# Last stream of an eight-phase kernel: more chunks of the down product split, weights turned earlier, one wait added on GpSimd

## The reference

```python
# phase 6: 16 heads of 8; half of the heads see every second row and are upsampled
x = x + jnp.tanh(g_xattn[3]) * _L3_xattn_ref(_layernorm(x), ctx_1024, ctx_1024, ...)
# phase 7: 32 experts of width 64, the best 8 (in the best 4 of 8 groups), and a shared expert of width 128
logits = h @ gate_w.T ; scores = sigmoid(logits) ; combine = 2.5 * normalised top 8
g = silu(einsum('th,eih->tei', h, w_gate)) ; u = einsum('th,eih->tei', h, w_up)
routed = einsum('tei,ehi->th', g * u * combine[:, :, None], w_down)
shared = (silu(h @ sh_gate.T) * (h @ sh_up.T)) @ sh_down.T
x = x + jnp.tanh(g_ffn[3]) * (routed + shared)
```

## Time and profile before

| | |
|---|---|
| three runs, median (lowest to highest) | 833.05 us (830.68 to 836.3) |
| the profiled execution | 832.02 us, of which the span is 830.0 us |
| PE, DVE, POOL, ACT busy | 802.3, 499.0, 450.2, 439.2 us (97, 60, 54, 53% of the span) |
| mean granted PE clock | 0.994 of full speed |
| phase 7 on PE | from 668.40 us to the end |

### The profile page before, as it was taken

The page is one execution under the profiler, slowest core; times in us unless marked ns, Lnnn a source line. Parts: engine busy times, 40 slices in busy tenths (PEclk is TensorE's granted clock), DMA queues, the critical chain, the costliest instruction groups (busy, mean ns, idle before and its releaser), DMA issues.

```text
span 830.0 us, 13575 instructions
## 1 busy us (share of the span) xinstructions
PE 802.3 (97%) x4407; PEld 557.1 (67%) x4407; DVE 499.0 (60%) x1419; ACT 439.2 (53%) x801; POOL 450.2 (54%) x432
## 2 busy tenths in 40 slices
PE   4999999999999999999999999999998999999998
PEld 4876667677767666665666666656564576677776
DVE  6865535393845545335555858676756647486744
ACT  2443555656546343324667676756654654546543
POOL 5375655466654536375546444354554357575463
PEclk9999999999999999999999999999998999999999
DMA  8303030315423242442234141312213042515161
GB/s 317 111 27 103 6 97 1 109 58 161 140 66 101 53 136 67 137 122 49 71 97 106 51 108 40 100 48 58 60 43 95 10 143 65 152 54 167 54 183 60
DMA packets 44871, 75.29 MB, mean 91 GB/s; under 512 B 8993, under 2 KB 9633, under 8 KB 44673
## 3 DMA queue, kind: packets, MB, share of 16 engines
q1 hardware_dynamic: 44656, 74.42, 30.5%
q10 hardware_dynamic: 144, 0.01, 0.0%
HBM read 56.11 MB, written 1.51 MB: 69 GB/s over the span
## 4 chain that ended last, share of the span: by engine, by line
PE 86%; DVE 8%; ACT 2%; issue 2%; POOL 1%; DMA 1%; SPq 0%; DVEq 0%; ACTq 0%
PE Y L979 17%; PE B L892 11%; PE B L894 11%; PE B L893 11%; PE B L1641 5%; PE B L1660 4%; PE B L1622 3%; PE B L1628 3%; DVE mxh L1930 2%; PE B L1621 2%; PE T L1440 2%; DVE xhat L1913 1%; PE Y L971 1%; PE Y L970 1%; PE Y L969 1%
## 5 line engine op out<-in xcount | busy, mean ns | idle before, releaser
L1276 POOL TENSOR_TENSOR shared<-shared,bcs 128x512 f32<-128x512 f32 x192 | 247.3, 1294 | 201.0 <-DVE shared L1336 147.6
L1130 ACT ACTIVATE shared<-B 128x512 f32<-128x512 f32 x204 | 121.7, 599 | 204.3 <-PE B L894 203.3
L1336 DVE TENSOR_TENSOR shared<-shared,B 128x512 f32<-128x512 f32 x168 | 114.8, 686 | 171.8 <-PE B L894 132.3
L979 PE MATMUL Y<-shared,down_lo 128*128 128x512 f32 x336 | 172.0, 595 | 0.0
L1870 POOL TENSOR_TENSOR shared_r<-shared_r,const 128x512 fp32r<-128x512 f32 (+1 forms) x128 | 115.5, 933 | 80.8 <-PE B L1622 54.6
L1930 DVE TENSOR_REDUCE mxh<-B 128x4 fp32r<-128x512 f32 (+1 forms) x128 | 78.7, 618 | 82.7 <-PE B L1622 81.6
L1796 ACT ACTIVATE shared<-B 128x512 f32<-128x512 f32 (+1 forms) x128 | 69.5, 543 | 67.5 <-PE B L1628 66.3
L1807 ACT COPY shared<-B 128x512 f32<-128x512 f32 (+1 forms) x128 | 64.5, 504 | 24.7 <-PE B L1641 24.7
L892 PE MATMUL B<-shared_r,gate_hi 128*128 128x512 f32 x102 | 75.1, 736 | 0.0
L1641 PE MATMUL B<-const,shared 128*128 128x128 f32 x448 | 72.0, 278 | 0.2 <-ACT shared L1807 0.2
L892 PE MATMUL B<-x_lo_r,gate_hi 128*128 128x512 f32 x102 | 70.7, 693 | 0.4 <-ACT shared L1130 0.4
(11 more groups left out here) (328 smaller groups left out, 1533.7 us busy)
## 6 DMA issues: line engine op xcount, KB each, us to landing
bcs<-wrow SPq DMA_DIRECT2D x96, 256.0 KB, 3.7
shared_r<-shared_r SPq DMA_DIRECT2D x256, 64.0 KB, 2.0
bcs<-wrow SPq DMA_DIRECT2D x128, 128.0 KB, 3.1
gate_lo<-in_moe SPq DMA_DIRECT2D x9, 256.0 KB, 5.4
up_lo<-in_moe SPq DMA_DIRECT2D x9, 256.0 KB, 6.1
down_lo<-in_moe SPq DMA_DIRECT2D x9, 256.0 KB, 3.9
small<-in_small SPq DMA_DIRECT2D x1, 1372.5 KB, 11.7
X<-in_x SPq DMA_DIRECT2D x4, 256.0 KB, 5.3
```

What stands on the lines that cost most here:

```text
L979: nc.tensor.matmul(Y[:], w_raw[2][:, at:at + P], hid[(n0 + c) % HIDDEN], start=(i == 0), stop=(i == m["NC"] - 1))\
L1130: nc.scalar.activation(sg[(n0 + n) % ACTIVE], B[n % GATES][:], ACT.Silu).then_inc(sem("sg_ready"), 1)
L1276: gp.tensor_tensor(by_weight, by_weight, bcs[(PLACE.k0[p] + r // m["PER"]) % BROADCAST], ALU.mult)\
L1336: nc.vector.tensor_tensor(hid[(n0 + n) % HIDDEN], sg[(n0 + n) % ACTIVE], up[:], ALU.mult)\
```

## The change

Four things change. The down product is split from chunk 2 of groups 1 to 3 on (`WHOLE` 5 becomes 2): nine more chunks are split. For this the high part of the down weights becomes three chunks wider; a first piece is cast in chunk 9 and its low part made in chunk 14, and the second piece is cast in chunk 10. The tiles behind it move by one. In phase 7 the routing weights are turned at i=13 instead of i=15 (`turn` also carries ACT's copy and SP's transfers with it). In cycle 6 POOL waits, between `power` and key tile 1 of cycle 7, until DVE has written the normalised rows.

```diff
-        WHOLE, HIGHS = 5, 10
+        WHOLE, HIGHS = 2, 10
         late = Area()
         down_hi = late.at_tile(15, [P, (MOE[7]["NC"] - WHOLE) * P], shared_r)
-        hid_hi = [late.at_tile(18 + i, [P, TG], shared_r) for i in range(HIGHS)]
+        hid_hi = [late.at_tile(19 + i, [P, TG], shared_r) for i in range(HIGHS)]
...
-            return slice((a - WHOLE) * P, (b - WHOLE) * P)
+            return slice((max(a, WHOLE) - WHOLE) * P, (b - WHOLE) * P)
+
+        def down_raw(q):
+
+            a, b = PIECES[7][q]
+            return slice(max(a, WHOLE) * P, b * P)
...
-                        table = dict(xt=1, logits=4, result=LAG + 3, turn=NC - 2 if MOE[to]["GK"] else NC - 3)
+                        table = dict(xt=1, logits=4, result=LAG + 3, turn=NC - (4 if to == 7 else 2) if MOE[to]["GK"] else NC - 3)
...
-                    if (g, i) == (1, a):
-                        pe.wait_ge(sem("down_lo_ready"), q)
+                    if (g, i) == (1, max(a, WHOLE)):
+                        pe.wait_ge(sem("down_lo_ready"), q + 1)
...
-        DOWN_ACT = {9: 1, 11: 2, 13: 3}
-        DOWN_POOL = {18: 1, 22: 2, 26: 3}
+        DOWN_ACT = {9: 0, 10: 1, 11: 2, 13: 3}
+        DOWN_POOL = {14: 0, 18: 1, 22: 2, 26: 3}
...
                 if c + 2 == CYCLES:
                     power(S4 + CYCLES)
+                    pool.wait_ge(sem("xhat_ready"), S4 + CYCLES + 1)
```

More of the change, by code:

```diff
@@ L1137, in stream_act @@
                     act.wait_ge(sem(f"raw1_{q}"), 96)
-                    nc.scalar.copy(down_hi[:, down_piece(q)], w_raw[2][:, piece(7, q)])\
+                    nc.scalar.copy(down_hi[:, down_piece(q)], w_raw[2][:, down_raw(q)])\
                         .then_inc(sem("down_hi_ready"), 1)
@@ L1280, in stream_pool @@
                     q = DOWN_POOL[n]
-                    c = piece(7, q)
-                    pool.wait_ge(sem("down_hi_ready"), q)
+                    c = down_raw(q)
+                    pool.wait_ge(sem("down_hi_ready"), q + 1)
                     after_down(pool, 7, 0, PIECES[7][q][1] - 1)
```

## The result

The changed kernel takes 835.68 us (median of 22 runs, 833.24 to 839.08), the kernel before 831.37 us beside it (22 runs). The ratio is 1.0056 (95% interval 1.0044 to 1.0067): slower by 4.7 us (4.3 by the two medians), within the 1% that was forecast. The two errors cancel, so the near hit of the time is luck. So the terms have to be read one by one.

What follows compares the result with a forecast made beforehand. PE, busy 97% of the span, was taken as the bound. From the profiled 832.0 us, -5.0 - 1.5 + 6.8 + 2.1 = +2.4 gave 834.4, or 835.4 from the median; forecast 835 us, range 826 to 840.

Steps and rivals of the forecast that it cites:

- all signs named for it: Normalising about 1.1 us, clock up in cycle 7, 45 split products, new PE waits at the turn, earlier `w_row` copy.
- Rivals C and D: C: normalising slow or key tile late, 839.4 us, chance 0.08; D: PE waits for low parts, 838 to 840, 0.10.
- The subtraction for the low part of x in cycle 7: DVE's step at t=2 may meet the moved key tile, taking up to 1.0 us from the gain of POOL's wait.
- The turn's waits: PE waits for `comb` or added X in three group transitions of phase 7: +6.8 us (4.3 to 7.3).
- Rival A: DVE comes in time for the turn: 826 to 827 us by the profile, 827 by the median; chance 0.26.
- The clock in the stream: In phase 7, one clock fall after PE's waits at the turn, +2.1 us (0 for none, 4 to 6 for two).
- Rival B: Waits of 2.5 and 3.4 us both drop the clock, up to 3.4 us each: 839, 840 by median; chance 0.10.
- POOL's wait: In cycle 7, faster normalising on DVE and no clock fall: -2.9 - 2.1 = -5.0 us.
- 4.05 - 1.11: Cycle 7's four normalising DVE operations shrink from 4.05 us to cycle 1's 1.11: gain 2.9 us.
- The splits: Nine more split down products in phase 7 save PE 1.5 us (1.2 to 1.6).
- without it part 2 could stall: Without the earlier turn, the nine added splits could stall on late weights in chunks 2 to 4; no size given.

Runs made afterwards that it cites:

- turn at 15, low part of x ahead: Changed kernel with the turn back at chunk 15 and DVE's low part of x ahead of a split chunk's product; 832.55 us, 1.0021 against the kernel before.
- turn behind the down product: Changed kernel with the turn at chunk 14 and, in phase 7's turn chunks, PE's down product ahead of it; 828.74 us, 0.9963 against the kernel before.

## Why the prediction was right, and where its steps were not

- **Direction, range and path:** right. The change loses by waits of PE at the turn, as forecast, and all signs named for it came, with two falls of the clock for the one that was counted. Rivals C and D did not show: the normalising became fast, and PE waits for no low part. The subtraction for the low part of x in cycle 7, to which up to 1.0 us was given, takes 0.68 us before and after.
- **The turn's waits:** 2.5, 3.4 and 0.9 us forecast, 2.48, 2.72 and 0.52 measured. The first is exact. In the second the lower value holds because only one term was real: PE came earlier by the splits, while routing and DVE were not later by the 0.45 us that I had added for ACT's cast. Measured from the start of chunk 27, PE's slot comes 0.45 us sooner with the splits (8.95 to 8.50 us), and X is added at 11.4 us with and without them. The kernel with only the turn moved, where the wait was 2.3 us, agrees with that. Rival A (DVE in time) is refuted.
- **The clock in the stream:** one fall of 2.1 us forecast. The profile shows two, one behind 2.48 and one behind 2.72 us of idle time. Their cost can be read from the starts of chunks 14, 15, 31 and 32, against the kernel with the turn back at 15, which has the same splits: 6.17 + 2.88 + 6.40 + 2.54 against 2.26 + 2.26 + 2.10 + 2.10 is 9.3 us. Of these 5.2 are the waits and 0.9 the transposes that moved here; 3.2 us are left for the two falls. Rival B's falls were half as long as it said. The waits were forecast 1.1 us too high (6.8 against 5.7) and the clock 1.1 too low (2.1 against 3.2), so that the sum of the two, 8.9 us, is met by luck. With the turn alone they cost 7.2 us in the timed runs and 8.4 in the stream, where the forecast's own rows without the splits give 2.5 + 2.5 + 2.1 = 7.1.
- **POOL's wait:** the mechanism is shown, in the profile and alone. The size was wrong, -5.0 forecast against -3.2 and -2.2 measured. The mis-sized terms are "4.05 - 1.11" and the clock fall behind it: I took the one profiled execution for the usual one. In the profiles of the three other versions without the wait the operations took 2.56 us and PE idled for 1.38; the clock fell there too.
- **The splits:** PE's part is right. Chunks 28 to 31 start 2.25 + 2.68 + 2.24 + 2.48 = 9.65 us behind the ones before them in the kernel before, and 2.48 + 2.52 + 2.10 + 2.10 = 9.20 with the turn at 14. The other two groups give 0.50 and 0.44 us, in all 1.4 us, of 1.5 forecast. With the turn at 14, 0.6 of it is left in the stream. But "without it part 2 could stall" stood there without a price: it is 4.8 us (from -1.4 to +3.4 with the splits alone). The sum did not need it, since the turn did move. Yet it is what makes the two edits one: neither is good without the other.
- **The sum:** in the two profiles it comes out. POOL's wait gives -5.2 us, and 5.7 of waits, 3.2 of clock and -1.4 of the splits make 7.5 of the 7.8 us by which the stream is longer. In the timed runs -3.2 (POOL) and +7.2 (turn) leave +0.7 for the splits in a total of +4.7, but each ratio is uncertain by about 1 us, so this says little. By the streams with the turn at 13 (157.75 to 157.18) the splits are worth -0.6: the third wait and the longer second one take 0.9 of their 1.4 us. The forecast's +2.4 was low mainly by POOL's wait, -5.0 in place of -3.2.

## What to carry to other kernels

An engine that never waits pays for every new wait in full; read the slot of a moved step and the end of what it needs as two times from the same timeline, as here 696.70 and 699.19, before moving it. Where one edit needs data sooner and another makes it late, look for the place between: one chunk later in the turn was worth about 7 us. And a long wait that comes from two engines meeting is a matter of their phase; one profile may show the best or the worst of it, so count how often it happens before taking its length as the gain.

## What the runs showed of the hardware

From 40 us on the granted clock fell behind each idle time of PE of 1.99 us and more (1.99, 2.26, 2.34, 2.46, 2.48, 2.72 and 3.56 us). It stayed behind 0.7 us, and directly behind the 1.07 us of cycle 7 in all thirteen profiles. Between these the idle time alone does not decide. Behind 1.38 us it fell in all three profiles that have it; behind 1.60 us in chunk 42 of the kernel "turn at 15, low part of x ahead" it stayed. And one wait of 1.6 us at 455 to 458 us stands in all thirteen profiles: behind it the clock stayed in twelve and fell in one, that of the changed kernel with the turn at 14. A row of PE's timeline and one of the clock behind it, for the kernel before and then for that one:

```profile
454.85 0.39 PE L1621 MATMUL B<-maskb,constb 128*128 128x512 bf16 x1 [1.61 <-ACT shared L1796]
456.00:462.00 6.00, 5.96 (x55) 4.12 (x55) 5.78 (x28) 3.91 (x8) 3.42 (x4) 1.00 0.27 92
```

```profile
456.19 0.39 PE L1626 MATMUL B<-maskb,constb 128*128 128x512 bf16 x1 [1.62 <-ACT shared L1801]
458.00:462.00 4.00, 4.00 (x28) 2.37 (x28) 3.34 (x21) 1.71 (x3) 1.01 (x1) 0.59 0.22 73
```

In two profiles with POOL's wait (turn back at 15; turn behind the down product) the clock fell for 3.5 us between 655 and 661 us, with no idle time of PE above 0.1 us in the 8 us before; in the seven others it stayed there. What decides is open. The kernel with only the splits, at cycle 7, behind 1.38 us:

```profile
630.00:636.00 6.00, 5.95 (x41) 3.48 (x40) 4.84 (x11) 2.87 (x10) 4.85 (x6) 1.00 0.32 78
636.00:642.00 6.00, 4.68 (x20) 3.27 (x21) 2.56 (x4) 2.34 (x5) 2.85 (x3) 0.60 0.41 101
642.00:648.00 6.00, 6.00 (x49) 4.26 (x48) 2.67 (x4) 3.86 (x10) 2.34 (x4) 0.83 0.38 90
```

I had taken 1.07 us, which kept the clock, as a mark for what is safe, and 1.38 has lost it here. Four DVE operations on SBUF data took 1.10 us alone, 2.56 with POOL's tile beginning inside them and 4.05 with both beginning together; their row maxima from PSUM, 0.41 to 0.69 us, took the same in all three.
